# Key copies of the first and last groups and the split of the expert weights on GpSimd, one softmax scaling on VectorE, in a fused audio tower

## The reference

```
h = relu(einsum('blfd,fd,fdk->blk', windows(x, 8), filt, W_k) + b_k)     # 248 positions, 64 features
n = layernorm(h); q, k, v = n @ Wq.T + bq, n @ Wk.T + bk, n @ Wv.T + bv
mask = (q[:, :, 0] != 0) & (k[:, :, 0] != 0)                             # one value per row
p = where(mask, softmax(q @ k.T / 8), 0)
h = h + (p @ v) @ Wo.T + bo
m = layernorm(h); the 2 best of 8 experts by m @ Wg + bg + bias, softmax over these two
h = h + sum over the two of weight * (relu(m @ W1[e] + b1[e]) @ W2[e] + b2[e])
```

## Time and profile before

| what | value |
|---|---|
| median of 3 runs | 299.21 us (298.03 to 301.09) |
| the profiled execution's own time | 298.85 us |
| its span, first to last instruction | 297.1 us |
| busy PE, DVE, ACT, POOL | 279.3, 241.1, 238.9, 103.8 us |
| key copies on SP's queue | 16, 248 KB each, 3.0 us median from issue to landing |

### The profile page before, as it was taken

How to read it: one execution, slowest core, us unless ns; L and a number is a source line. 1 busy time by engine, 2 the same in 40 slices (tenths; PEclk the granted TensorE clock), 3 DMA queues, 4 the chain that set the end, 5 groups by cost and what they waited for, 6 DMA issues and landing times.

```text
span 297.1 us, 6188 instructions
## 1 busy us (share of the span) xinstructions
PE 279.3 (94%) x1737; PEld 200.4 (67%) x1737; DVE 241.1 (81%) x890; ACT 238.9 (80%) x549; POOL 103.8 (35%) x99
## 2 busy tenths in 40 slices
PE   7776999999999999999999999999998999998993
PEld 6544657777777768677777777686776675665572
DVE  2576669989897979889898979798898899895666
ACT  3449598898998889898989989898887788876762
POOL 2204023442536162443415351715342151506051
PEclk9998899999999999999999999999999999999999
DMA  6430206061433526170624426250605133242301
GB/s 189 108 96 9 73 34 176 4 172 57 114 113 76 152 71 158 37 191 4 164 65 109 118 71 159 71 155 31 163 2 130 45 104 89 87 105 69 91 19 34
DMA packets 12785, 27.58 MB, mean 93 GB/s; under 512 B 3152, under 2 KB 5456, under 8 KB 12752
## 3 DMA queue, kind: packets, MB, share of 16 engines
q1 hardware_dynamic: 12464, 26.91, 33.8%
q10 hardware_dynamic: 288, 0.28, 0.3%
HBM read 20.85 MB, written 2.27 MB: 78 GB/s over the span
## 4 chain that ended last, share of the span: by engine, by line
PE 69%; DVE 12%; DMA 7%; issue 5%; ACT 4%; POOL 1%; POOLq 0%; SPq 0%; DVEq 0%; ACTq 0%
PE bank_y L1379 15%; PE bank_a L1290 11%; PE bank_h L1363 7%; PE bank_h L1364 7%; PE bank_s L1307 5%; PE bank_s L1419 4%; DMA kk<-kk 4%; PE bank_s L1318 4%; PE bank_s L1386 3%; DVE acc L820 3%; PE bank_b L1390 2%; PE bank_s L1390 2%; PE bank_s L1440 2%; PE bank_b L1386 2%; PE bank_b L1430 1%
## 5 line engine op out<-in xcount | busy, mean ns | idle before, releaser
L465 ACT ACTIVATE hid<-bank_h,col 128x496 f32<-128x496 f32 x128 | 84.3, 672 | 10.8 <-PE bank_h L1364 7.1
L374 POOL TENSOR_TENSOR p<-p,rmask 124x496 f32<-124x496 f32 x32 | 32.5, 1016 | 97.9 <-DVE rmask L863 97.7
L1379 PE MATMUL bank_y<-hid,w_sb 128*64 128x248 f32 x508 | 63.7, 380 | 0.8 <-DVE acc L820 0.7
L1363 PE MATMUL bank_h<-xs,w_hi 128*128 128x496 f32 x128 | 58.1, 454 | 0.2 <-DVE xs L256 0.2
L820 DVE SCALAR_TENSOR_TENSOR acc<-bank_y,col,cb 128x248 f32<-128x248 f32 x127 | 53.1, 468 | 4.7 <-PE bank_y L1379 1.9
L1364 PE MATMUL bank_h<-xs,w_lo 128*128 128x496 f32 x128 | 49.5, 387 | 0.0
L1379 PEld LDWEIGHTS bank_y<-hid,w_sb 128*64 128x64 f32 x508 | 32.8, 136 | 24.7 <-issue 11.2
L268 POOL TENSOR_TENSOR total<-acc 128x496 f32<-128x496 f32 x16 | 20.0, 1251 | 46.1 <-DVE acc L820 45.9
L456 ACT ACTIVATE p<-bank_s,nmax 124x248 f32<-124x248 f32 x64 | 29.3, 464 | 2.3 <-DVE nmax L852 1.1
L388 POOL TENSOR_TENSOR x_lo<-x,x_hi 128x512 fp32r<-128x512 f32 x16 | 20.6, 1291 | 24.9 <-ACT x_hi L524 24.9
L1363 PEld LDWEIGHTS bank_h<-xs,w_hi 128*128 128x128 f32 x128 | 24.1, 189 | 7.0 <-issue 3.6
(11 more groups left out here) (120 smaller groups left out, 545.8 us busy)
## 6 DMA issues: line engine op xcount, KB each, us to landing
cb<-weights SPq DMA_DIRECT2D x60, 248.0 KB, 3.9
kk<-kk SPq DMA_DIRECT2D x16, 248.0 KB, 3.0
x<-xt SPq DMA_DIRECT2D x15, 256.0 KB, 3.5
out<-h SPq DMA_DIRECT2D x16, 124.0 KB, 3.7
w_sb<-w SPq DMA_DIRECT2D x3, 256.0 KB, 4.0
wtok_sb<-wtok SPq DMA_DIRECT2D x1, 256.0 KB, 2.7
x<-xt ACTq DMA_DIRECT2D x1, 256.0 KB, 3.8
weights<-ct_sb SPq DMA_DIRECT2D x15, 15.5 KB, 1.4
```

Source lines behind the costliest of these rows:

```text
L374: pool.tensor_tensor(p_sb[b][0:HALF, :, :], p_sb[b][0:HALF, :, :], rmask[0:HALF, b, :].unsqueeze(2).to_broadcast([HALF, 2, WIN]), ALU.mult ...
L465: act.activation(hid[2 * (p % 2) + s][:, :], bank_h[s][:, 0:TOK], ACT.Relu, bias=col[:, C_B1 + e:C_B1 + e + 1]).then_inc(hid_ready[s], 1)
L1363: pe.matmul(bank_h[e % 2][:, 0:TOK], w1_hi[:, e, :], xs[m % 2][:, :], start=True, stop=False)
L1379: last = pe.matmul(dst[b * D:b * D + D, :], w2_sb[:, 2 * p + s, :], hid[2 * (p % 2) + s][:, b * WIN:(b + 1) * WIN], start=True, stop=True)
```

## The change

In groups 0, 1, 2, 13, 14 and 15 the keys are no longer copied by a transfer: POOL copies the high part when it is there (`copy_high`), then the low part (`copy_low`), each with 64 partitions by 496 elements, and counts both in a new semaphore `k_moved`, which `scores` waits for in these groups. Behind `copy_low` POOL waits for its own copy to be complete. Groups 3 to 12 keep the transfer.

`expert_high` and `expert_low` move from DVE to POOL, behind the key copies of group 0 and ahead of its `scale(0, 0)`.

In group 0 the second p is scaled on DVE (`scale_first`, behind `masked_recip(0, 1)` and ahead of `low_tokens(1, 0)`), not by POOL; `turn_p(0, 1)` waits for it on a semaphore of its own, and the count of `p_ready` that others wait for is lower by one.

```
+        KEYS_FROM, KEYS_TO = 3, 13
+        def moved(n):
+            return 2 * (n if n < KEYS_FROM else n - KEYS_TO + KEYS_FROM)
 SP, fill:
                 load(2)
-                copy_keys(0)
                 load(3)
                 load(4)
-                copy_keys(1)
                 load(5)
                 store_weights(0)
                 spread(0, 0)
-                copy_keys(2)
                 spread(0, 1)
 SP, drain: copy_keys(13), copy_keys(14) and copy_keys(15) go, each from between two spreads
 POOL:
+            def copy_high(n):
+                pool.wait_ge(kh_ready, n + 1)
+                after(pool, sc_done, 2 * n)
+                if n >= KEYS_TO:
+                    pool.wait_ge(k_copied, 16 * (KEYS_TO - KEYS_FROM))
+                if n < KEYS_FROM:
+                    pool.wait_ge(xl_ready, min(n + 3, 5))
+                else:
+                    pool.wait_ge(fold_ready, n - 2)
+                pool.tensor_copy(kk[0:D, 0, :], kk[D:128, 0, :].bitcast(F32)).then_inc(k_moved, 1)
+            def copy_low(n):
+                pool.wait_ge(kl_ready, n + 1)
+                pool.wait_ge(k_moved, moved(n) + 1)
+                pool.tensor_copy(kk[0:D, 1, :], kk[D:128, 1, :].bitcast(F32)).then_inc(k_moved, 1)
+                pool.wait_ge(k_moved, moved(n) + 2)
 expert_high and expert_low: the same two functions with pool in dve's place
 POOL, fill:
                 low_inputs(2)
+                copy_high(0)
+                copy_low(0)
+                expert_high()
+                expert_low()
                 scale(0, 0)
-                scale(0, 1)
                 low_inputs(3)
+                copy_high(1)
+                copy_low(1)
                 scale(1, 0)
                 scale(1, 1)
                 low_inputs(4)
+                copy_high(2)
+                copy_low(2)
                 add(pool, 0, 1)
                 scale(2, 0)
 POOL, drain:
                 fold_halves(10)
+                copy_high(13)
+                copy_low(13)
                 add(pool, 11, 1)
...
                 fold_halves(11)
+                copy_high(14)
+                copy_low(14)
                 add(pool, 12, 1)
...
                 fold_halves(12)
+                copy_high(15)
+                copy_low(15)
                 scale(15, 0)
 DVE:
             def recip(n, b):
                 dve.wait_ge(ex_ready, 2 * n + b + 1)
-                after(dve, p_ready, 2 * n + b - 1)
+                after(dve, p_ready, 1 if n == 1 else 2 * n + b - 2)
+            def scale_first():
+                dve.wait_ge(rm_ready, 2)
+                dve.tensor_tensor(p_sb[1][0:HALF, :, :], p_sb[1][0:HALF, :, :],
+                                  rmask[0:HALF, 1, :].unsqueeze(2).to_broadcast([HALF, 2, WIN]),
+                                  ALU.mult).then_inc(p_first, 1)
 DVE, fill:
                 low_keys(0)
-                expert_high()
                 low_queries(0)
                 keep_values(0)
                 masks(0)
-                expert_low()
...
                 masked_recip(0, 1)
+                scale_first()
                 low_tokens(1, 0)
 PE:
             def scores(n, b):
-                pe.wait_ge(k_copied, 16 * n + 16)
+                if KEYS_FROM <= n < KEYS_TO:
+                    pe.wait_ge(k_copied, 16 * (n - KEYS_FROM) + 16)
+                else:
+                    pe.wait_ge(k_moved, moved(n) + 2)
             def turn_p(n, b):
-                pe.wait_ge(p_ready, 2 * n + b + 1)
+                if n == 0:
+                    pe.wait_ge((p_ready, p_first)[b], 1)
+                else:
+                    pe.wait_ge(p_ready, 2 * n + b)
```

More of the change, by code:

```diff
@@ L191, in audio_tower @@
         k_copied = sem("k_copied")
+        k_moved = sem("k_moved")
+        p_first = sem("p_first")
         v_done = sem("v_done")
@@ L342, in drain @@
                 spread(11, 0)
-                copy_keys(13)
                 spread(11, 1)
@@ L348, in drain @@
                 spread(12, 1)
-                copy_keys(14)
                 store_weights(13)
@@ L352, in drain @@
                 spread(13, 0)
-                copy_keys(15)
                 spread(13, 1)
@@ L382, in fold_halves, with expert_high, expert_low @@
                 pool.tensor_tensor(both[:, :], total[:, 0:WIN], total[:, WIN:TOK], ALU.add).then_inc(fold_ready, 1)
+            def copy_high(n):
[13 more added lines that the diff above has]
+                pool.wait_ge(k_moved, moved(n) + 2)
+            def expert_high():
+                pool.wait_ge(par_moe, 16 * N_MOE)
+                pool.tensor_copy(w1_hi[:, :, :], w1_sb[:, :, :]).then_inc(set_moe, 1)
+            def expert_low():
+                pool.wait_ge(set_moe, 1)
+                pool.tensor_tensor(w1_lo[:, :, :], w1_sb[:, :, :], w1_hi[:, :, :].bitcast(F32),
+                                  ALU.subtract).then_inc(set_moe, 1)
             def low_inputs(d):
@@ L791, in value_weights @@
                 last.then_inc(set_val, 1)
[L793 to L801, removed]
             def weigh(m, p):
```

## The result

Over 22 executions the changed kernel takes 296.79 us in the median (295.24 to 298.24), the kernel before 298.08 us beside it. The ratio is 0.9946, 95% interval 0.9923 to 0.9968: 1.6 us faster (298.08 x 0.0054), for 1.7 forecast. The two medians themselves lie 1.3 us apart; a few long executions of before, of 300.04 us and more, count for more in the ratio than in the median. The profiled execution is the longest of them: 298.24 us, span 296.4, mean granted clock 0.987.

The account below looks back on a forecast made before the run. PE bounds the middle, so gains come only where the chain leaves it, in start and drain. Start -1.35, group 2 +0.5, drain -0.85 sum to -1.7 on 298.85: 297.15, as median 297.5 us; range 295.2 to 300.0.

Parts of the forecast that it names:

- start up to scale(0,0): Group 0: key copies and expert splits on POOL let scale(0,0) start at 23.3 for 24.46, gain 1.15 us.
- second p: Group 0: scaling the second p on VectorE takes 0.68 us and gives the next step's inputs earlier, gain 0.2 us.
- group 2: POOL's copies push add(0,1) over the xs subtractions; cost between 0 and 1.0 us, taken as +0.5.
- drain: Groups 13 to 15 at the end: -0.6 from group 13, -0.25 from group 14, 0 from group 15, together -0.85 us.
- Group 1: Copies end at about 32.1, but scores(1,0) at 35.4 waits for the logits either way: nothing gained.
- rmask's wait behind expert_low: Start, group 0: rmask, moved to about 22.95, meets expert_low on POOL and waits until 23.1.
- The price of a copy: POOL's one-input copies taken at half the two-input slope: 0.72 us for 496 elements, 1.27 for 1024.
- The hold: VectorE operations with two SBUF inputs wait until a running POOL operation ends; one that starts ahead of it passes.
- The slower rival: Mask loses to expert_low in group 0, and to add(0,1) in group 2, or copies are slow: 300.3 us; chance 0.20.
- Group 15: Drain: scores waited for logits, kmask is held 0.15 us, low_queries keeps its place: 0, or +0.3 at the upper copy price.
- group 13: Drain: POOL's copies end near 228.2, in time, removing PE's idle wait for the keys: -0.6 us.
- The rival: Clock stays up at 29 to 30 us, where its fall costs about 1.9 us: 295.6 us; chance 0.17.

Follow-up runs that it names:

- start-alone kernel: Kernel before with only the start changed (keys of groups 0 to 2 and both expert splits on POOL, second p on VectorE): 297.57 us, ratio 0.9996.
- the one with group 2 by transfer: The changed kernel with group 2's keys copied by a transfer again: 296.37 us, ratio 0.9948 to before.
- the version that keeps PE busy: The changed kernel plus products on zeros, which nobody reads, in PE's gaps of the start: 295.39 us, ratio 0.9921 to before.
- the two kernels with added products: Changed kernel and kernel before, each with the same products on zeros in PE's gaps of the start: 295.39 us and 297.02 us.

## Why the prediction was right

**The sum.** The forecast was 297.5 us, in a range from 295.2 to 300.0, and a gain of 1.7; measured were 296.79 us and a gain of 1.6 by the ratio, 1.3 by the medians. The level had some luck: 297.5 started from a median of before of 299.21, of three executions, where 22 have 298.08. By its terms, in stages at full clock where the clock bears on them:

| term | forecast | stages |
|---|---|---|
| start up to scale(0,0) | -1.15 | 6.39 - 7.60 = -1.21 |
| second p | -0.2 | 3.47 - 3.69 = -0.22 |
| group 2 | +0.5 | 0.07 + 0.32 = +0.39 |
| drain | -0.85 | 53.54 - 54.47 = -0.93; -0.4 to -1.2 by execution |

The stages add up to -1.97, or -1.4 to -2.2 with the drain's scatter, around the 1.6 to 1.7 of the totals. Group 1 was forecast as nothing, and attend(0) to gate 0, in which it lies, takes 7.27 to 7.29 us at full clock with its key copies on POOL and without.

**The start** went by the steps named. On the time axis of before (0.13 us off the changed kernel's) low_queries started at 18.69 for 18.70 forecast and scores(0,0) at 19.88 for 20.1, mask passed, and scale(0,0) started at 23.25 for 23.3. Mask passed by less than the forecast had: 0.02 us ahead of w_lo for 0.08. But the order was the same in all eight traces with w_lo on POOL and nothing put in mask's way. The forecast put rmask's wait behind expert_low at 23.1; that wait did not occur, as the copies were shorter than the value taken for them.

**The price of a copy**, half way between two ends, was too high: 0.59 for 0.72 us, 1.04 for 1.27. w1_lo by the two-input slope was right (2.39 for 2.35). The prediction's estimate by the Trainium skill (GPSIMD Engine Reference, Elementwise: side-by-side cycle accounting), from its cycles an element and the fixed 0.20 us of the rows, was 0.63 and 1.08; the trace agrees with it, within 0.04 us.

**The hold.** That it is there, both for the subtraction of xs in group 2 and for rmask, is shown. The slower rival rested on where it begins, and the argument from two starts, 0.09 us ahead and 0.03 behind, holds in every trace but one: mask was held in group 15 at 0.03 behind, and passed in group 0 at 0.25 behind when a long write stood ahead of it. The Trainium skill (GPSIMD Engine Reference, Key points) names the VectorE forms that contend; the trace agrees, with rmask at 1.97 us and xs at 1.19.

**Group 15** was forecast as "kmask is held 0.15 and low_queries keeps its place". As the copies were shorter, POOL's second copy lay across mask and not between: 0.42 us held, 0.21 of it on the path (31.40 less 31.19). The drain's gain comes out as forecast all the same, since group 13 gave 0.81 for 0.6.

**The clock** was the term that the sum left out and that only a rival had, on one side. It lies on the other. The forecast held the fall as it was. In the changed kernel's profile it came earlier, at 25.8 us for 28.1, and stayed longer, and cost 2.5 us for 1.4: (3.95 + 9.30) - (3.47 + 7.27) = 2.51 and (3.69 + 8.66) - (3.68 + 7.28) = 1.39. That explains the profiled execution, which is only 0.6 us ahead of before. The rival priced the fall of before at about 1.9 us, for the 1.39 measured. Neither the fall nor its length belongs to a kernel: the start-alone kernel, with the same start, had the 3.4 us of before in its profile, the one with group 2 by transfer none. With a mean clock of 0.999 or more the medians are 297.04 (21 of 60 executions of before measured beside these experiments) and 295.36 (4 of 22 of the changed kernel): 1.7 us apart. At 0.994 they are 298.41 (23) and 296.63 (4), 1.8 apart. Below 0.9925 there are 13 of the 60 and 13 of the 22. So the change gives about its 1.7 us at equal clock, the lower clock takes some back where it falls more often, and the version that keeps PE busy gets the rest: 295.39 us. That the fall depends on PE's idleness in the start is shown by the two kernels with added products: 9 of 9 and 11 of 12 of their executions have a mean clock of 0.996 or more, for 5 of 22 of the changed kernel and 23 of 60 of before without them. Why it comes more often in the changed kernel, whose PE is busy 7.3 of the 10 us from 16 to 26 for 6.4 before, is not.

**What stays open:** why mask passed 0.25 us behind POOL's start when a long write stood ahead of it; and the 0.07 us between gate 0 and kmask 2.

## What to carry to other kernels

Work that is moved to GpSimd is paid for on VectorE as well: list what VectorE does with two SBUF operands while the moved work runs, and place it where VectorE reads PSUM. A gain in a latency-bound start is worth what the clock leaves of it, so look at the granted clock behind the idle stretch, and try a few products on zeros in PE's gap; here they gave 1.1 to 1.4 us by themselves. Where executions scatter by more than the effect, compare stages between two marks in the timeline instead of totals: 0.2 us can be seen there, while in the ratios over 12 executions 0.4 us could not be told.

## What was not expected of the hardware

- The hold between VectorE and GpSimd works both ways: a GpSimd copy of 0.60 us took 1.12 beside a VectorE cast that had started 0.03 us ahead.
- An operation of two elements a partition was held 1.97 us by a 2.34 us subtraction, and ended 0.02 us behind it; yet a small one 0.25 us behind another such start, behind a plain write, took 0.10 us, the only one of its kind in fourteen traces.
- The same start had, from one execution to another, no fall of the clock, one of 3.4 us (27.6 to 31.0) and one of 6.8 us (25.8 to 32.6), and the longest cost 2.5 us of time. Three products of 128 columns and one of 64, on zeros, kept the clock up in the start.
- The same 248 KB key copy landed 3.5 to 5.1 us behind its issue for groups 13 and 14, and 2.9 to 3.1 for groups 0, 1, 2 and 15.
